# A decoder kernel on one core: younger pair first in four woven stages, one table set in a router, expert weights on another queue

## What is computed

```python
def _layernorm(x, axis=-1, eps=1e-05):
    m = jnp.mean(x, axis=axis, keepdims=True)
    v = jnp.var(x, axis=axis, keepdims=True)
    return (x - m) / jnp.sqrt(v + eps)

x = x + _L0_ffn_ref(_layernorm(x), ...)    # 8 experts, top 2, router by _sinkhorn
x = x + _L1_attn_ref(_layernorm(x), ...)   # flow attention, 16 heads of 8
x = x + _L1_ffn_ref(_layernorm(x), ...)    # quantised gate/up/down, inner width 512
x = x + _L2_attn_ref(_layernorm(x), ...)   # linear attention with relu, rope and rms norms
x = x + _L2_ffn_ref(_layernorm(x), ...)    # 8 experts, top 2
x = x + _L3_attn_ref(_layernorm(x), ...)   # block attention, blocks of 64

def _sinkhorn(log_alpha, iters=3):         # in _L0_ffn_ref, with temperature 0.5
    for _ in range(iters):
        log_alpha = log_alpha - jax.nn.logsumexp(log_alpha, axis=-1, keepdims=True)
        log_alpha = log_alpha - jax.nn.logsumexp(log_alpha, axis=-2, keepdims=True)
    gates = jnp.exp(log_alpha)
    return gates / (jnp.sum(gates, axis=-1, keepdims=True) + 1e-08)
```

## Time and profile before

| | before |
|---|---|
| median of 3 runs | 1985.57 us (1977.89 to 1986.81) |
| the profiled execution | 1987.53 us, its span 1985.7 us |
| busy: PE, PEld, DVE, ACT, POOL | 1468.4 (74%), 894.7 (45%), 1222.3 (62%), 934.6 (47%), 380.2 us (19%) |
| mean granted TensorE clock | 0.85 |
| DMA | 84.52 MB, of which 35.93 MB are POOL's gathers |

### The profile page before, as it was taken

One profiled execution on the slowest core, in us unless ns is written; L12 is line 12 of the kernel. 1 busy time (PEld: TensorE's weight loads), 2 busy tenths in 40 slices (PEclk: granted clock), 3 DMA queues, 4 the chain that ended last, 5 costly groups with the idle time before them and its releaser, 6 DMA issues. The chain is left out here.

```text
span 1985.7 us, 32127 instructions
## 1 busy us (share of the span) xinstructions
PE 1468.4 (74%) x11270; PEld 894.7 (45%) x11270; DVE 1222.3 (62%) x4051; ACT 934.6 (47%) x2009; POOL 380.2 (19%) x404
## 2 busy tenths in 40 slices
PE   5997978844763669996446599999974993677874
PEld 2554434433551443443224356666654882443432
DVE  7776378844233647776666477777664223557876
ACT  4554266642221235554632177777752440126655
POOL 3320021013645005320011000000002546002100
PEclk9999999965995779999557599999995995669995
DMA  3320023112451003320010000000003662003300
GB/s 117 57 44 2 0 34 48 23 32 64 140 120 36 1 26 64 52 44 19 0 55 1 11 6 7 6 7 12 1 8 91 203 182 56 1 16 44 54 2 21
DMA packets 58686, 84.52 MB, mean 43 GB/s; under 512 B 8352, under 2 KB 46496, under 8 KB 58016
## 3 DMA queue, kind: packets, MB, share of 16 engines
q1 hardware_dynamic: 48384, 46.54, 11.5%
q0 software_dynamic: 10144, 35.93, 6.4%
HBM read 51.18 MB, written 9.18 MB: 30 GB/s over the span
## 5 line engine op out<-in xcount | busy, mean ns | idle before, releaser
L638 DVE TENSOR_REDUCE maxs<-ps 128x4 f32<-128x1024 f32 x192 | 234.8, 1223 | 62.5 <-PE ps L966 60.9
L794 ACT ACTIVATE L_xattn_probs<-ps 128x1024 f32<-128x1024 f32 x192 | 196.5, 1024 | 85.1 <-PE ps L991 80.8
L3386 ACT ACTIVATE wide_pr<-wide_sc,wide_nm 128x256 f32<-128x256 f32 x256 | 126.9, 497 | 12.7 <-DVE wide_nm L3321 12.2
L966 PE MATMUL ps<-keys,L_xattn_qs 64*128 64x256 bf16 x768 | 75.3, 274 | 38.4 <-DVE maxs L638 31.9
L1007 PE MATMUL ps<-L_xattn_probs,values 128*32 128x256 f32 x1536 | 102.8, 385 | 0.0
L3293 DVE CUSTOM_DVE_ANT_0 wide_sc<-ps,wide_mask 128x256 f32<-128x256 f32 x256 | 93.8, 420 | 9.6 <-PE ps L3411 8.6
L3316 DVE COPY wide_prT<-ps 128x512 f32<-128x512 f32 x64 | 44.3, 692 | 83.0 <-PE ps L3424 82.8
L1484 POOL DMA_INDIRECT moe_xs<-normed,moe_table x92 | 86.8, 944 | 28.0 <-issue 28.0
L991 PE MATMUL ps<-L_xattn_qm,keys 64*128 64x256 bf16 x768 | 74.6, 271 | 7.3 <-ACT L_xattn_probs L794 7.0
L1890 DVE SCALAR_TENSOR_TENSOR moe_z_sb<-ps,moe_wt,moe_a_sb 128x256 f32<-128x256 f32 x46 | 22.3, 484 | 89.8 <-ACT moe_a_sb L1922 77.1
L3331 DVE TENSOR_SCALAR wide_pr<-wide_pr,wide_inv 128x256 f32<-128x256 f32 x256 | 75.5, 349 | 1.8
(11 more groups left out here) (641 smaller groups left out, 3798.5 us busy)
## 6 DMA issues: line engine op xcount, KB each, us to landing
keys<-L_xattn_k_parts SPq DMA_DIRECT2D x108, 64.0 KB
L_xattn_qs<-L_xattn_q_parts SPq DMA_DIRECT2D x108, 64.0 KB
expert_out<-moe_y SPq DMA_DIRECT2D x46, 128.0 KB
weights<-in_packed_L_xattn SPq DMA_DIRECT2D x2, 1316.0 KB, 7.5
keys<-L_attn_k_parts SPq DMA_DIRECT2D x36, 64.0 KB
L_attn_qs<-L_attn_q_parts SPq DMA_DIRECT2D x36, 64.0 KB
normed<-moe_xn SPq DMA_DIRECT2D x2, 1024.0 KB, 4.8
wide_mask<-in_mask SPq DMA_DIRECT2D x8, 256.0 KB, 2.8
```

The costliest lines, as they stand in the source:

```text
L638: v.tensor_reduce(nm, ps[:, BANK_M:BANK_M + 2, :].rearrange("p j (t n) -> p j t n", t=2), AX.X, ALU.max, negate=True).then_inc(S("m_used"), 1)
L794: a.activation(probs[:, s % RING, :, :, :].rearrange("p j t n -> p j (t n)"), ps[:, BANK_P:BANK_P + 2, :], ACT.Exp, scale=HD ** -0.5)\
L966: mm = pe.matmul(ps[:, BANK_M + j, c + c0:c + c1], qs[half[j], m % 2, gp, q0:q0 + P], kk[half[j], m % 2, gp, b * SEQ + c0:b * SEQ + c1], s ...
L3386: ins = a.activation(pr[:, s % 3, j, qt, :], sc[:, s % 2, j, qt, :], ACT.Exp, bias=nm[:, s % 2, n:n + 1], accum_out=sums[:, s % 2, n:n + 1])
```

## The change

It has three parts, and the hunk of `weave_ahead` applies to DVE of flow and block:

```diff
-def weave(units, phases, lag):
+def weave(units, phases, lag, later_first=False):
-    units = list(units)
+    units = list(enumerate(units))
     for t in range(phases + lag * (len(units) - 1)):
-        for m, unit in enumerate(units):
+        for m, unit in units[::-1] if later_first else units:
             if 0 <= t - lag * m < phases:
                 next(unit, None)
 def weave_ahead(fronts, ahead, units, phases, lag):
-        for m, unit in enumerate(units):
+        for m, unit in units[::-1]:
...
     def fetch(self, g):
-        def weights(j):
-            if j >= BUFS:
-                g.wait_ge(S("y_ready"), j - BUFS + 1)
-            g.indirect_dma_start(self.wt[:, j % BUFS, :], None, self.experts,
-                                 bass.IndirectOffsetOnAxis(self.rows_of[:, j:j + 1], 0))\
-             .then_inc(C.routed[f"w_loaded_{j % BUFS}"], 16)
-        def rows(j):
+        g.wait_ge(S("normed_stored"), 16)
+        g.wait_ge(S("table_ready"), 1)
+        for j in range(SLICES):
             if j >= BUFS:
                 g.wait_ge(S("x_turned"), j - BUFS + 1)
...
-        g.wait_ge(S("rows_ready"), 1)
-        weights(0)
-        g.wait_ge(S("normed_stored"), 16)
-        g.wait_ge(S("table_ready"), 1)
-        rows(0)
-        weights(1)
-        rows(1)
-        for j in range(2, SLICES):
-            weights(j)
-            rows(j)
+    def weights(self, sp, j):
+        row = sp.value_load(self.rows_of[0:1, j:j + 1], min_val=0, max_val=7 * P)
+        sp.dma_start(self.wt[:, j % BUFS, :], self.experts[bass.ds(row, P), :])\
+          .then_inc(self.C.routed[f"w_loaded_{j % BUFS}"], 16)
     def keep(self, sp):
+        sp.wait_ge(S("rows_ready"), 1)
+        for j in range(BUFS):
+            self.weights(sp, j)
         for j in range(SLICES):
             sp.wait_ge(S("y_ready"), j + 1)
             sp.dma_start(C.expert_out[j * SLICE:(j + 1) * SLICE, :].rearrange("(h p) d -> p h d", p=P),
                          self.y[:, j % 2, :].rearrange("p (h d) -> p h d", d=D)).then_inc(C.routed[f"y_stored_{j % 2}"], 16)
+            if j + BUFS < SLICES:
+                self.weights(sp, j + BUFS)
...
             def _(a):                                   # sinkhorn_moe, the ACT program
+                a.preload_act_table_set("natural_log_exp_and_others")
...
-                weave([pair(m) for m in range(PAIRS)], PHASES, LAG)
+                weave([pair(m) for m in range(PAIRS)], PHASES, LAG, later_first=True)
```

## The result

| | before | changed |
|---|---|---|
| median of the runs | 1982.32 us | 1929.95 us (1923.05 to 1935.05) |
| ratio | | 0.9729 (95% interval 0.9697 to 0.9762) |
| profiled execution, its span | 1987.53, 1985.7 us | 1927.86, 1926.0 us |

A forecast was written before the change was run, and what follows sets the result against it. No engine fills the woven stages; chains through the engines' written order set their length. Terms 6.9 + 7.5 + 11.4 + 10.5 - 3 - 8 = 25.3 us took 1987.5 to 1962.2 us, range 1945 to 1984.

The forecast's parts named there:

- Experts' steady state: Expert slices: nothing gained, since weights are never last; slices stay at 4.4 and 4.8 us.
- The starts: Starts of both expert stages: rows issued and turned earlier, 7.5 us less with later row waits, bounds 3 to 9.
- SP's loop: Expert slices: wait, store, register load (taken as 1 us) and weights issue stay under 2 us of 4.4.
- Rival (a): Expert slices: SP's loop becomes the slice and weights come late; at 6 us per loop, 2024 us; chance 0.08.
- Flow: Flow's shared cycles: q/k/v 5.3 us earlier, 1.5 given back; 3.8 per cycle, 11.4 us less, bounds 3 and 14.
- Block: Block's cycles: q/k/v and DVE3 go earlier, 3.5 us per cycle, 10.5 us less in three, bounds 6 and 13.
- Relu: Relu's cycles: DVE10 runs later and DVE5 follows it; 1 us per cycle, 3 us lost, bounds 1 to 5.
- Bit: Bit's cycles: younger pair's DVE0 delays the older's second half; 2.7 us per cycle, 8 lost, bounds 5 to 9.
- Tables: Router: table loads before the logs vanish, 6.9 us less, bounds 5.6 to 6.9, or nothing if loads stay.
- Rival (d): First pairs of flow, block: waits without releaser go, about 10 us each (0.10), or grow by as much (0.05).

The follow-up runs named there:

- e14_third_gather: Changed kernel, plus a third POOL gather per slice into a buffer nothing reads: 1958.96 us against 1982.91 for the kernel before, ratio 0.9885.
- e8_best: Changed kernel with bit's old order and SP's third and fourth weights held until two slices' rows are turned: 1882.23 us against 1931.60 for the kernel before.
- e6_after_again: The changed kernel, unchanged, on a chip without the waits: 1896.61 us against 1931.60 for the kernel before, ratio 0.9822.
- e5_before_again: The kernel before, unchanged, profiled again on a chip without the waits: 1931.64 us.
- e13_paced_returns: Kernel before with POOL's return gathers paced by one more wait, on a chip with the waits: 1950.89 us against 1982.91, ratio 0.9832.
- e16_sp_weights_2: Kernel before with only the expert weights moved to SP, on a chip with the waits: 1969.08 us against 1982.91, ratio 0.9926.

## Why the prediction was wrong

**Experts' steady state: the step that failed.** It said "nothing gained", because up starts 0.48 us after the copied rows in every slice. That is true and was the wrong end to look at: the copy itself was late, by ACT's waits for PE's turn, 10.7 us of them without a releaser. The mean of 4.4 us hid that many slices take about 3.6 us and the others 4.2 to 7.0. POOL's part was dismissed as "an engine that is idle half the time". That counts 0.95 us per gather; with the 0.30 between two, three gathers take 3.75 us, more than a slice of 3.6. The term was put at nothing and measured 16.2 us: with two gathers the waits are gone, with three they are back (e14_third_gather), and 18.6 us with them. In the slices of `top2_moe` three gathers in 4.8 us bring no such wait.

**The starts: the gain did not come.** The rows were to gain the 2.5 us of issue. They were issued earlier and landed no earlier: four weights transfers are on the DMA engines at the same time, and with two of them held back the turns do come earlier (e8_best). PE in the changed kernel, the turns of the first two slices in each expert stage:

```profile
471.02 0.69 PE L1508 MATMUL ps<-const,moe_xs 128*128 128x128 f32 x2 [7.39 <-DMA moe_xs<-normed,moe_table]
473.52 0.69 PE L1508 MATMUL ps<-const,moe_xs 128*128 128x128 f32 x2 [1.80 <-DMA moe_xs<-normed,moe_table]
```

```profile
1481.80 0.69 PE L1508 MATMUL ps<-const,moe_xs 128*128 128x128 f32 x2 [7.94 <-DMA moe_xs<-normed,moe_table]
1486.38 0.69 PE L1508 MATMUL ps<-const,moe_xs 128*128 128x128 f32 x2 [3.89 <-DMA moe_xs<-normed,moe_table]
```

The first stage's second turn is 9.4 us behind `rows_ready` as before; the second stage's is now 12.0 us behind it (1474.34 to 1486.38), before 10.9 (1518.26 to the 1529.12 of rows 7). The Trainium skill (DMA: Bandwidth & Descriptors, "Issuing engines are not separate DMA queues") has transfers of all queues interleave on the same engines. These traces agree: with two weights transfers fewer at that time, the first up matmul, which stands behind the second turn, comes 1.7 and 2.3 us earlier (e8_best against e6_after_again).

The 1.2 us that the first stage lost to its first result are something else. That result is copied 1.3 us after its matmuls ended:

```profile
482.38 0.42 DVE L1735 COPY moe_y<-ps 128x256 f32<-128x256 f32 x1 [1.31 <-PE ps L1814]
```

In e6_after_again DVE copies it at once, and there the stretch is 1.5 us shorter than in e5_before_again. In `top2_moe` it is longer by 1.2 to 1.4 us on both kinds of chip.

**SP's loop.** Rival (a) is ruled out. The first four weights issues start at 465.16, 466.68, 467.79 and 468.89: one register load and one issue take 1.1 us (the first 1.5), 0.34 of it the issue, so the load is about 0.8; the estimate was 1. The four in one row:

```profile
465.16 4.07 SPq L1485 DMA_DIRECT2D moe_wt<-in_packed_experts  x4
```

**Flow: right mechanism, too small.** The last shared cycle of the changed kernel, PE, DVE and ACT, against rows 9:

```profile
655.42 3.78 PE L2192 MATMUL ps<-flow_scaled,const 128*128 128x256 f32 x8 [3.21 <-DVE flow_scaled L2094]
...
660.90 0.32 PE L2207 MATMUL ps<-flow_qkv_parts,flow_pick 96*128 96x384 bf16 x1 [0.84 <-ACT flow_hT L2152]
...
664.31 1.11 PE L2230 MATMUL ps<-flow_vc,flow_tokens 128*128 128x128 f32 x8
...
667.00 1.89 PE L2192 MATMUL ps<-flow_tokens,const 128*128 128x256 f32 x8
```

```profile
669.62 1.29 DVE L2070 SCALAR_TENSOR_TENSOR flow_prod<-flow_tokens,flow_totals 128x512 f32<-128x512 f32 x2 [1.73 <-ACT flow_totals L2143]
```

Counted from the start of the older pair's scaled sums (655.42 here, 691.89 before), q/k/v comes after 5.5 us where it was 10.5, 5.0 earlier, and the forecast had 5.3. The totals come after 11.6 where it was 17.8, 6.2 earlier and not 3.8: nothing was given back, because q/k/v takes 3.2 us and not the 5.2 to 6.7 that the forecast allowed, and PE8 takes 1.3 in place of 2.8. Over the shared cycles the granted clock went from 0.76 to 0.89:

```profile
639.00:719.00 80.00, 49.02 (x202) 37.37 (x203) 50.11 (x136) 22.43 (x39) 0.00 (x0) 0.76 0.00 1
```

```profile
617.00:674.00 57.00, 40.97 (x200) 30.48 (x198) 47.94 (x130) 22.01 (x39) 0.00 (x0) 0.89 0.00 1
```

(before, then changed). And the flows start 2.6 us behind the totals where it was 4.1, since ACT's attention copy and DVE's add of the older pair no longer stand between them; the forecast had not priced that edge. In all, the cycle (from one L2099 to the next, L2094 in the changed kernel) is 7.7 us shorter here and 6.4 and 7.0 in the two others; the term of 3.8 was about half of it. How much of it is the clock alone and how much order was not separated; e6_after_again shows 5 us between two clocks in one and the same stage.

**Block: right, a little more.** The changed cycle, against rows 10:

```profile
1669.52 1.15 PE L2698 MATMUL ps<-const,blocks_xn 128*128 128x128 f32 x4 [2.24 <-DVE blocks_xn L246]
1670.60 2.40 PE L2729 MATMUL ps<-blocks_kv,blocks_qT 128*64 128x160 f32 x16
1672.93 3.29 PE L2703 MATMUL ps<-weights,blocks_hT 128*128 128x384 f32 x8
...
1680.46 4.80 PE L2714 MATMUL ps<-blocks_vv,blocks_kx 64*128 64x129 f32 x16 [1.96 <-ACT blocks_vv L2674]
```

q/k/v stands directly behind the attention and takes 3.3 us, before 5.2. The cycles lose 3.4, 4.6 and 3.4 us, 3.5 was the forecast; 2.5 more come at the last pair's end.

**Relu: wrong sign.** Counted from the start of DVE5 (1037.38 before, 999.14 changed), DVE10 does begin 3.1 us later and DVE5 of the younger pair stands directly behind it, as forecast; but DVE0 of the younger pair is 2.5 us earlier by the same edit, ahead of the older pair's attention, and the forecast did not count it. The two nearly cancel in the first two cycles, and the last gains 1.4.

**Bit: right, a little less.** 2.0 us per cycle by the starts of the product, and 5.9 in all (2.7 and 8 forecast). DVE0's 2.36 us stand ahead of the second half:

```profile
949.87 1.11 DVE L246 TENSOR_SCALAR bit_xn<-x,mv,rstd 128x128 f32<-128x128 f32 x4
...
952.23 1.41 DVE L2837 SCALAR_TENSOR_TENSOR bit_h<-ps,bit_usc,bit_gate 128x512 f32<-128x512 f32 x2
```

**Tables: right**, 6.9 forecast and 6.9 between the start of the router and `table_ready` in the two traces (8.2 at `table_ready`, of which 1.2 stood before the router began).

**The range.** It was built from the costs in one profile of one chip. Stage by stage the profiles gained more than forecast in the slices (16.2 us), in flow (9.6), relu (4.8), block (3.4), bit (2.1) and the rest (8.4), and less only in the two starts (10.1). Rival (d) named the waits without a releaser, but as something in flow and block that a change of order might move; there they stayed. Where none are, the change is 35.0 us, which the range of 3.5 to 42.5 us less would have held, but not for the reasons given: flow's and block's terms are too small there as well, and the starts' is not there.

## What to carry to other kernels

A wait that the trace gives no releaser for is a cost with an owner: collect all of them, the short ones too, and note what the other engines issue at that time, before an even-looking mean is read as a rate. Where work is woven, the order has to be turned in every queue that the chain passes (in flow, ACT's or PE's alone each cost 0.2 to 0.3%), and it pays only where the younger pair's work was queued behind a wait of the older; where it filled a gap, as in bit, it costs nearly its own length each cycle (2.0 of 2.4 us). A transfer issued early on another queue still takes its bandwidth from the small one that is needed first.

## What the hardware showed that was not expected

- On some of the chips used, ACT and DVE start up to 12.4 us behind the end of the matmuls that they wait for while POOL issues indirect gathers one after the other; the kernel before takes about 50 us of 1980 more there, and on two other chips the same kernel has none of it. Pacing the gathers (e13_paced_returns) or issuing fewer (e16_sp_weights_2) takes it away, one more per slice (e14_third_gather) brings it back. What in the chip holds the result, and whether rate or an unbroken run of gathers decides, stays open: e14_third_gather has pauses of 1.7 us between its threes and still shows it, while the slices of `top2_moe` with three in 4.8 us do not and only its start, where POOL issues without a pause, has one of 3.1 us.
- TensorE's granted clock in a woven stage is not a constant of the stage: 0.73 and 0.79 for one and the same flow, 5 us apart, and it rose from 0.76 to 0.89 over the shared cycles when the order left fewer gaps (PE busy 49.0 of 80.0 us, then 41.0 of 57.0).
